# Attention mask added to the scores in PSUM by VectorE, from a tile that GpSimd makes, in place of bf16 products on TensorE and row tiles made by ScalarE

## The reference

```
qkv = (x @ W_qkv).reshape(B, N, HEADS, 3, DIM_HEAD)
dots = jnp.einsum('bhid,bhjd->bhij', q, k) * scale
m2 = mask[:, None, :, None] & mask[:, None, None, :]
dots = jnp.where(m2, dots, -big)
attn = jax.nn.softmax(dots, axis=-1) * LA
adj = jnp.where(m2, adjacency_mat[:, None], 0.0)
dist = jnp.where(m2, distance_mat[:, None], big)
attn = attn + LG * adj + LD * jnp.exp(-dist)
out = jnp.einsum('bhij,bhjd->bhid', attn, v)
return out @ W_out + b_out
```

## Time and profile before

| | us |
|---|---|
| median of three runs | 1293.99 (1293.24 to 1295.88) |
| profiled execution: span from first to last instruction | 1291.5 |
| PE busy | 1247.2 (97%) |
| weight load busy | 1110.3 (86%) |
| DVE busy | 1068.8 (83%) |
| ACT busy | 971.6 (75%) |
| POOL busy | 478.5 (37%) |
| granted clock of TensorE, mean | 0.993 |

### The profile page before, as it was taken

The page is one execution under the profiler, slowest core; times in us unless marked ns, Lnnn a source line. Parts: engine busy times, 40 slices in busy tenths (PEclk is TensorE's granted clock), DMA queues, the critical chain, the costliest instruction groups (busy, mean ns, idle before and its releaser), DMA issues.

```text
span 1291.5 us, 32910 instructions
## 1 busy us (share of the span) xinstructions
PE 1247.2 (97%) x9589; PEld 1110.3 (86%) x9589; DVE 1068.8 (83%) x3399; ACT 971.6 (75%) x2806; POOL 478.5 (37%) x1126
## 2 busy tenths in 40 slices
PE   6799999999999999999999999999999999999985
PEld 5688888888888888888898888898888898888874
DVE  3688888888888898888898888888888888888885
ACT  5477877777877777877777787778787777787773
POOL 3233444333443333443333343333343433344432
PEclk9899999999999999999999999999999999999998
DMA  6000100000000000000000100000001000000000
GB/s 214 17 8 21 26 25 25 16 16 18 25 25 25 22 11 17 25 25 25 25 9 17 25 25 25 25 8 19 23 25 25 25 8 23 20 25 25 17 9 9
DMA packets 44293, 32.52 MB, mean 25 GB/s; under 512 B 8176, under 2 KB 43120, under 8 KB 44272
## 3 DMA queue, kind: packets, MB, share of 16 engines
q1 hardware_dynamic: 42688, 31.47, 8.4%
q0 software_dynamic: 176, 0.52, 0.2%
q10 hardware_dynamic: 1408, 0.27, 0.1%
HBM read 23.87 MB, written 8.39 MB: 25 GB/s over the span
## 4 chain that ended last, share of the span: by engine, by line
PE 93%; DVE 3%; ACT 1%; issue 1%; DMA 1%; POOL 0%; DVEq 0%; SPq 0%; POOLq 0%; ACTq 0%
PE PS L405 15%; PE PS L406 15%; PE PS L409 15%; PE PS L494 5%; PE PS L548 5%; PE PS L495 5%; PE PS L498 5%; PE PS L528 4%; PE PS L538 4%; PE PS L584 3%; PE PS L568 2%; PE PS L598 2%; PE PS L520 2%; DVE ysb L1447 1%; PE PS L611 1%; PE PS L604 1%
## 5 line engine op out<-in xcount | busy, mean ns | idle before, releaser
L1722 POOL TENSOR_TENSOR rs<-mv,eps_c 128x1 f32<-128x1 f32 x256 | 61.2, 239 | 582.9 <-DVE mv L1208 581.4
L1726 POOL TENSOR_TENSOR rs<-rs,mhalf 128x1 f32<-128x1 f32 x320 | 176.3, 551 | 25.3
L891 ACT ACTIVATE prob<-PS,neg_max 128x128 f32<-128x128 f32 x512 | 179.7, 416 | 2.0 <-DVE neg_max L1272 2.0
L1285 DVE SCALAR_TENSOR_TENSOR prob<-prob,rl,gate 128x128 f32<-128x128 f32 x512 | 145.6, 347 | 1.5
L494 PE MATMUL PS<-xT_hi,wqk_hi 128*128 128x256 f32 x512 | 141.3, 297 | 0.0
L495 PE MATMUL PS<-xT_hi,wqk_lo 128*128 128x256 f32 x512 | 134.9, 285 | 0.0
L891 ACT ACTIVATION_READ_ACCUMULATOR prob<-PS,neg_max 128x1 f32 x512 | 131.4, 257 | 0.0
L1319 DVE SCALAR_TENSOR_TENSOR hid<-PS,Dn,b_bc 128x512 f32<-128x512 f32 x64 | 48.1, 751 | 85.4 <-PE PS L409 85.4
L498 PE MATMUL PS<-xT_lo,wqk_hi 128*128 128x256 f32 x512 | 103.5, 284 | 0.0
L494 PEld LDWEIGHTS PS<-xT_hi,wqk_hi 128*128 128x128 f32 x512 | 98.2, 192 | 5.3 <-issue 5.0
L495 PEld LDWEIGHTS PS<-xT_hi,wqk_lo 128*128 128x128 f32 x512 | 98.7, 193 | 0.0
(11 more groups left out here) (225 smaller groups left out, 4227.3 us busy)
## 6 DMA issues: line engine op xcount, KB each, us to landing
xin<-in_x_dram SPq DMA_DIRECT2D x32, 256.0 KB, 2.7
out_dram<-xout SPq DMA_DIRECT2D x32, 256.0 KB, 2.2
adj_in<-in_adj_dram SPq DMA_DIRECT2D x32, 128.0 KB, 2.1
wrow<-in_adj_dram SPq DMA_DIRECT2D x32, 128.0 KB, 4.5
wqkv_raw<-in_L_gnn_W_qkv_dram SPq DMA_DIRECT2D x1, 1536.0 KB, 7.6
w_raw<-in_L_gnn_W_dram SPq DMA_DIRECT2D x3, 512.0 KB, 11.4
mask_bc<-in_nodemask_dram SPq DMA_DIRECT2D x32, 32.0 KB, 2.8
wk_raw<-in_L_gnn_Wk_dram SPq DMA_DIRECT2D x3, 256.0 KB, 9.0
```

The lines of the kernel that those rows point to most:

```text
L891: last = act.activation(prob[:, t, h, :], PS[:, bank, k * P:(k + 1) * P], ACT.Exp, bias=neg_max[:, t, h:h + 1], accum_out=row_sum[:, t, h: ...
L1285: last = dve.scalar_tensor_tensor(prob[:, t, h, :], prob[:, t, h, :], rl[:, t, h:h + 1], gate[:, t], ALU.mult, ALU.add)
L1726: return pool.tensor_tensor(rs[:, n, g, 1:2], rs[:, n, g, 0:1], mhalf[:], ALU.pow)
```

## The change

The bf16 row tiles, their two activations and the products of L520 go. The first product of q and k in each bank now starts the accumulation. POOL makes a tile `mbig` of 128 x 256 from `mbc`, once in a group, as mbc * 2^100 - 2^100: 0 where row and column are valid. DVE adds it to the scores of each graph in PSUM, for all 8 heads in one instruction, before the maximum, and the maximum waits for that. `mask_` on ACT waits for POOL to have read the `mbc` of the group before. Sixteen small memsets on POOL in the set-up go, and the constants that are waited for are 5 instead of 10.

```diff
@@ -80,14 +80,11 @@
-        mask_ab = at("mask_ab", [P, 4])
-        mrow_l = at("mrow_l", [P, G, P], BF16)
-        mrow_r = at("mrow_r", [P, G, P], BF16)
@@ -103,6 +100,7 @@
+        mbig = at("mbig", [P, G, P])
@@ -260,7 +258,7 @@
-        DVE_FSTEPS, DVE_BSTEPS, POOL_FSTEPS, POOL_BSTEPS = 4 + 3 * G, 1 + 8 * G, 1 + 2 * G, 7 * G
+        DVE_FSTEPS, DVE_BSTEPS, POOL_FSTEPS, POOL_BSTEPS = 4 + 4 * G, 1 + 8 * G, 1 + 2 * G, 7 * G
@@ -372,7 +370,6 @@
-                sp.wait_ge(act_mrow, i * 2)
@@ -514,19 +511,13 @@
                 last.then_inc(pe_AT, 1)
             def S_(i, t):
-                pe.wait_ge(act_mrow, i * 2 + 2)
-                for par in range(2):
-                    p = par * DH
-                    pe.matmul(PS[:, bank_S[t] + par, :], mrow_l[p:p + DH, t, :],
-                              mrow_r[p:p + DH, t:t + 1, :].to_broadcast([DH, HEADS // 2, P]),
-                              start=True, stop=False, skip_group_check=True)
                 for k in range(HEADS // 2):
                     if k % 2 == 0:
                         pe.wait_ge(act_qk, i * 4 + 3 + k // 2)
                     for par in range(2):
                         p = par * DH
                         last = pe.matmul(PS[:, bank_S[t] + par, k * P:(k + 1) * P], qk[p:p + DH, k, t, :],
-                                         qk[p:p + DH, QKB // 2 + k, t, :], start=False,
+                                         qk[p:p + DH, QKB // 2 + k, t, :], start=(k == 0),
                                          stop=(k == HEADS // 2 - 1), skip_group_check=True)
                 last.then_inc(pe_S, 1)
@@ -854,11 +845,8 @@
             def mask_(i):
                 act.wait_ge(m_in, i * 16 + 16)
-                act.wait_ge(pe_S, i * G)
                 act.wait_ge(pool_gate, i)
-                for dst, a in ((mrow_l, 0), (mrow_r, 2)):
-                    act.activation(dst[:].rearrange("p g n -> p (g n)"), mask_bc8[:], ACT.Identity,
-                                   bias=mask_ab[:, a + 1:a + 2], scale=mask_ab[:, a:a + 1]).then_inc(act_mrow, 1)
+                act.wait_ge(pool_mbig, i)
                 act.wait_ge(dve_mcol, i + 1)
                 for g in range(G):
                     act.activation(mbc[:, g * P:(g + 1) * P], mask_bc8[:, g * P:(g + 1) * P], copy,
@@ -1268,7 +1256,9 @@
                 def max_(t):
                     dve.wait_ge(pe_S, i * G + t + 1)
+                    dve.wait_ge(pool_mbig, i + 1)
                     scores = PS[:, bank_S[t]:bank_S[t] + 2, :].rearrange("p b (h n) -> p (b h) n", n=P)
+                    step.done(dve.tensor_tensor(scores, scores, mbig[:, t:t + 1, :].to_broadcast([P, HEADS, P]), ALU.add))
                     dve.tensor_reduce(neg_max[:, t], scores, AX_X, ALU.max, negate=True).then_inc(dve_max, 1)
                 def rl_(t, half):
@@ -1685,20 +1675,6 @@
-                pool.memset(mask_ab[:], 0.0).then_inc(pool_const, 1)
-                rows = 2
-                for base in (0, DH):
-                    for col, second in enumerate((1.0, 0.0, BIG, -BIG)):
-                        pool.wait_ge(pool_const, 6)
-                        last = pool.memset(mask_ab[base:base + rows, col:col + 1], second)
-                    last.then_inc(pool_const, 1)
-                pool.wait_ge(pool_const, 8)
-                for base in (0, DH):
-                    for col, first in enumerate((BIG, -BIG, 0.0, 1.0)):
-                        last = pool.memset(mask_ab[base:base + 1, col:col + 1], first)
-                    last.then_inc(pool_const, 1)
@@ -1746,10 +1722,18 @@
                     step.done(pool.tensor_tensor(gate[:], gate[:], adj_in[:], ALU.add))
                     pool.tensor_tensor(flat, flat, mbc[:], ALU.mult).then_inc(pool_gate, 1)
+                def mbig_():
+                    pool.wait_ge(act_mbc, i * G + G)
+                    pool.wait_ge(dve_max, i * G)
+                    settle(pool)
+                    pool.tensor_scalar(mbig[:].rearrange("p g n -> p (g n)"), mbc[:], BIG, -BIG, ALU.mult, ALU.add)\
+                        .then_inc(pool_mbig, 1)
                 def rs0_(t):
                     scale_shift(step, NORM0, t, dve_mv0, i * G + t + 1, 2.0).then_inc(pool_rs0, 1)
-                return step, resid_, gate_, rs0_
+                return step, resid_, mbig_, gate_, rs0_
             def back(j):
                 step = Steps(pool, pool_bstep, j, POOL_BSTEPS)
@@ -1781,12 +1765,14 @@
-                    fstep, fresid_, gate_, rs0_ = front(i)
+                    fstep, fresid_, mbig_, gate_, rs0_ = front(i)
+                if F:
+                    mbig_()
@@ -1813,10 +1799,11 @@
-                fstep, fresid_, gate_, rs0_ = front(0)
-                pool.wait_ge(pool_const, 10)
+                fstep, fresid_, mbig_, gate_, rs0_ = front(0)
+                pool.wait_ge(pool_const, 5)
+                mbig_()
```

More of the change, by code:

```diff
@@ L240, in gnn_stack_kernel @@
         (act_adjT, act_xT0, act_gate, act_qk, act_v, act_AT, act_exp, act_PT, act_OT,
-         act_adjTb, act_mrow, act_mbc, act_BHT, act_x1) = (
+         act_adjTb, act_mbc, act_BHT, act_x1) = (
             sem("act_" + n) for n in ("adjT", "xT0", "gate", "qk", "v", "AT", "exp", "PT", "OT",
-                                        "adjTb", "mrow", "mbc", "BHT", "x1"))
+                                        "adjTb", "mbc", "BHT", "x1"))
         (dve_xT0, dve_HT, dve_mcol, dve_Be, dve_Dsum, dve_Dn, dve_max, dve_attn, dve_OT, dve_y0, dve_mv0, dve_deg) = (
             sem("dve_" + n) for n in ("xT0", "HT", "mcol", "Be", "Dsum", "Dn", "max", "attn", "OT", "y0", "mv0", "deg"))
-        (pool_resid0, pool_gate, pool_rs0) = (sem("pool_" + n) for n in ("resid0", "gate", "rs0"))
+        (pool_resid0, pool_gate, pool_rs0, pool_mbig) = (sem("pool_" + n) for n in ("resid0", "gate", "rs0", "mbig"))
         (pe_ax, pe_h, pe_hT, pe_hw, pe_y1, pe_xT2, pe_Z01, pe_Z2, pe_si, pe_T1, pe_T2, pe_xT3, pe_Z3, pe_T3) = (
@@ L331, in set_up_done @@
             eng.wait_ge(set_small, N_SMALL)
-            eng.wait_ge(pool_const, 10)
+            eng.wait_ge(pool_const, 5)
             eng.wait_ge(ld_vec, 16 * 3)
@@ L1080, in first @@
                 adjT_(0)
-                act.wait_ge(pool_const, 10)
+                act.wait_ge(pool_const, 5)
                 mask_(0)
@@ L1171, in gate_vectors @@
                 dve.wait_ge(set_small, 3)
-                dve.wait_ge(pool_const, 10)
+                dve.wait_ge(pool_const, 5)
                 dve.tensor_tensor(gate_c[:, 0:1], bsum[:], ab_bc[:], ALU.add).then_inc(set_small, 1)
```

## The result

The changed kernel takes 1365.43 us (median of 4, 1365.08 to 1366.26), the kernel before beside it on the same chip 1293.62. The ratio is 1.0556, with a 95% interval of 1.0541 to 1.0571: 71.8 us slower, where 64 were forecast. The profiled execution took 1366.26 us, its span is 1364.5, against 1291.5 before.

What follows compares the result with a forecast made beforehand. PE was taken to bound the kernel, with DVE's run behind its wait for h having 0.50 us of slack. 31 groups at 2.1 us, 65.1, less 1.1 in the prologue: +64.0, 1294 to 1358 us; range 1335 to 1390.

Steps and rivals of the forecast that it cites:

- The mechanism: DVE's run from the second hid to `norm_(0, 1)`: only 0.50 us of slack against PE, and both additions lie inside it.
- The addition's size: DVE's addition of 128x1024 in PSUM: 1.22 us, with the following wait 1.26 us, two per group 2.52 us.
- Rivals A: DVE's addition collides with itself reading and writing the same PSUM banks, taking 2.4 us: about 1431 us; chance 6%.
- D: DVE's addition goes at the copy's rate, 0.7 us each: about 1325 us; chance 5%.
- the last decides: PE's new stalls in a group lie inside one another; the last, at the fifth transpose, moves from 616.10 to 618.18.
- 2.1 us per group: Each of 31 loop groups gets 2.1 us longer, to 40.6 us, 65.1 us in all.
- PE's gain: The removed pairs of products before the scores save PE 0.62 us per group, lost because this lies before the deciding stall.
- Rival C: The additions are hidden in DVE's wait for h and only PE's saving is left: 1274 us; chance 3%.
- The prologue: First group, another order: up to 1.6 us go from the chain ending at DVE's w2c; 1.1 us counted as won.
- ACT and POOL: ACT's two dropped activations count 0; POOL's added tile, 0.74 to 1.48 us, is done before DVE's first add and costs nothing.
- DVE's share of the chain rises to a third: Expected sign on the profile page: DVE's part of the chain that ended last goes from 3% to about a third.

Runs made afterwards that it cites:

- Experiments 3: Changed kernel with DVE's reduce `cnt_` moved ahead of the first hid, into the wait for h: 1356.63 us, ratio 1.0490.
- 4: Kernel before the change, with DVE's reduce `cnt_` moved ahead of the first hid, into the wait for h: 1293.63 us, ratio 0.9998.
- 7: Changed kernel with the additions replaced by SBUF-only ones of the same size, placed ahead of the first hid, scores unmasked: 1287.95 us, ratio 0.9950.
- Experiment 1: Changed kernel with DVE's two additions per group taken out, scores left without a mask: 1285.92 us, ratio 0.9947.
- Experiment 8: Changed kernel with DVE's hw pair moved ahead of the second graph's addition and maximum: 1428.61 us, ratio 1.1048.
- experiment 2: Kernel before the change, with POOL's tile and DVE's additions put in, bf16 products and row tiles kept: 1366.87 us, ratio 1.0567.
- experiment 10: Changed kernel with ACT's prologue copy of the first transposed probabilities moved ahead of the splits of weights: 1365.87 us, ratio 1.0555.
- experiment 11: Changed kernel with each DVE addition made twice in a row, so the mask is added two times: 1478.55 us, ratio 1.1420.

## Why the prediction was right, and where it was off

**The mechanism held.** DVE's run behind the wait for h had almost no slack against PE, and the two additions stand in it. Experiments 3, 4 and 7 show this from three sides: a shorter run gives time back, in the kernel before it gives none, and additions of the same size outside the run are almost free, 2.0 us where they cost 93.5 inside it.

**The addition's size held.** 1.228 us for 1.22, and 0.12 us for the wait behind it, where the overlap lost and the gap together were put at 0.13. Rivals A (1431) and D (1325) fall with that row. Experiment 1 gives 2.54 us per group for the two, against 2.52.

**The step "the last decides" failed in its choice.** I had the fifth transpose, with 0.50 us of slack, as the last stall, and wrote of y1 that it needs hw(0) of DVE. It needs both, and with 0.46 us of slack it decides. Experiment 8 takes the pair out of the way and the stall at y1 goes. The slack was nearly the same, so this alone costs 0.04 us per group.

**The term "2.1 us per group" was too small by 0.21**, 6.5 us in all. It was 2.52 + 0.06 - 0.50 = 2.08; the rows give 2.66 + 0.05 - 0.46 + 0.12 - 0.06 = 2.31. Too small were three parts: the slack, by the 0.04 above; the 0.12 that PE loses behind the stall, since the weights of y1 are what it waited for, which the sum had at nothing; and the way of the hw pair, 2.66 and not 2.52. The 0.06 that comes back in the rest goes against them. Of the 0.14 in the hw pair, 0.05 lies ahead of the run: the second hid starts 3.00 us after the group does, before 2.95. Another 0.07 stands in front of the first addition, which now waits for two semaphores where the reduce waited for one; I put that at 0. Before, the reduce started 0.11 us after the start of the aggregate (607.15, 607.26); now the addition starts 0.18 after it (640.87, 641.05), though nothing is listed as waited for. In experiment 1, where the additions are gone and the wait is left, it is 0.19. The second addition has the same two waits and loses nothing: it starts 0.58 us after the low part of hT (644.99, 645.57), the reduce of before 0.57 after it (609.94, 610.51). The row ahead of the first is 0.18 us long and that ahead of the second 0.66; that the longer row hides the extra wait fits these two places and was not tried apart.

**PE's gain**, "0.62 us per group, lost because it lies before the stall": lost it was (experiment 2), but it was 0.23 at most (experiment 1). Rival C's time of 1274 was out of reach even without additions.

**The prologue**, "1.1 us as won": 1.6 were lost in the profiled execution. I followed the chain to w2c and not what comes behind it, the wait for probT at 37.46 and the clock. With this term the span is 1355.5 + 6.5 + 2.7 = 1364.7, measured 1364.5; this closes the account of one execution and is no test of it. Where the clock held, the first hid of the loop came at 64.54 (experiment 2) and 65.55 (experiment 10), before at 64.97, so that the sign of this term without the clock stays open.

**ACT and POOL** cost nothing, as put. POOL's tile took 0.41 us and was ready at 638.79, over 2 us ahead of its use. The sentence that DVE's share of the chain rises to a third was wrong: 16%.

**What stays open.** Why PE's h takes about 0.04 us longer between the two hids (1.36 us before, 1.40 in the changed kernel and in experiment 1) was not found. That PE loses 0.1 us where its first weight load starts together with the product is read from rows, at y1 and at S, and was not tried apart; in experiment 8, where y1 has no stall, its row is 1.02 long again. Why 2.26 us of stall lets the clock fall and 1.04 does not was met, not varied in steps, and in the prologue 2.51 us did both.

## What to carry to other kernels

An engine's idle time is worth something only at the place where it lies: find the run of rows behind its last wait, and for each row of another engine that waits for this run write down the slack; work moved into the run costs its length less the smallest slack, however idle the engine is on the page. This holds as long as the clock does: in experiments 8 and 11 the longer stalls cost about 1 us per group beyond such a sum. Read from the code, not from names, how many results each wait asks for. Removing work from the bounding engine is to be priced by the distance of the starts of what follows it, since a part can come back there, as 0.10 of the 0.23 us of each pair did in experiment 1.

## What the runs showed of the hardware

- DVE adding a tile of SBUF to 128x1024 fp32 in PSUM in place takes 1.228 us, as long as reading the same columns (1.224).
- Stalls of PE of 0.90 and 1.04 us per group left the granted clock at 1.00; with 2.17 and 2.30 (experiment 11), and with 0.90 and 2.26 (experiment 8), it fell below 0.9 for some us in the group read, and the mean from 100 to 400 us was 0.97 and 0.98. In the prologue 2.51 us let it fall in the changed kernel and not in experiment 2.
- Two sources in SBUF beside POOL's work: DVE 1.69 instead of 1.22 us, POOL 1.60 instead of 0.73.
- A product whose first weight load starts together with it takes 0.1 us longer: 0.48 instead of 0.38 us at y1, 0.37 instead of 0.27 at S.
